# Adjacency loads of a two-layer GNN kernel: partition quadrants 2 and 3 issued by ScalarE instead of SyncE

## What is computed

```python
def reference(x, adj, L0_gnn_w, L1_gnn_W, L1_gnn_b):
    # layer 0
    A = adj + eye(N)
    d = rsqrt(sum(A, axis=1))
    h = elu(((A * d[:, None] * d[None, :]) @ x) @ L0_gnn_w)
    x = layernorm(x + h)
    # layer 1
    h = relu((adj @ x) @ L1_gnn_W.T + L1_gnn_b)
    return layernorm(x + h)
```

## Time and profile before

| | |
|---|---|
| median of 3 runs | 950.19 us (949.61 to 953.15) |
| the profiled execution, first to last instruction (its span) | 945.9 us |
| time outside the span (median less span) | 4.3 us |
| TensorE busy | 798.6 us, 84% of the span |
| VectorE busy | 736.0 us, 78% |
| ScalarE busy | 530.9 us, 56% |
| GpSimd busy | 101.9 us, 11% |
| granted TensorE clock, mean | 0.951 of full speed |
| moved by DMA | 190.08 MB, mean 201 GB/s |
| SP's queue | 187312 packets, 185.23 MB |

### The profile page before, as it was taken

One profiled execution on the slowest core, in us unless ns is written; L12 is line 12 of the kernel. 1 busy time (PEld: TensorE's weight loads), 2 busy tenths in 40 slices (PEclk: granted clock), 3 DMA queues, 4 the chain that ended last, 5 costly groups with the idle time before them and its releaser, 6 DMA issues. The chain is left out here.

```text
span 945.9 us, 10551 instructions
## 1 busy us (share of the span) xinstructions
PE 798.6 (84%) x3524; PEld 656.8 (69%) x3524; DVE 736.0 (78%) x537; ACT 530.9 (56%) x1192; POOL 101.9 (11%) x108
## 2 busy tenths in 40 slices
PE   0151756569989999999999999999999999999993
PEld 0041635457768888888888888888887778888882
DVE  0454636579979878989898898988987979888861
ACT  2153535367777764475676757667573665455352
POOL 0000000000000000021110211202110231122020
PEclk9995777788999999999999999999999999999997
DMA  9999999999999999998999999999999799998900
GB/s 215 221 219 221 221 220 220 221 225 238 228 230 227 203 206 216 208 219 180 199 209 197 201 207 193 212 191 220 195 211 212 171 211 209 219 219 181 198 23 22
DMA packets 191972, 190.08 MB, mean 201 GB/s; under 512 B 6960, under 2 KB 191920, under 8 KB 191920
## 3 DMA queue, kind: packets, MB, share of 16 engines
q1 hardware_dynamic: 187312, 185.23, 96.2%
q10 hardware_dynamic: 4608, 4.20, 1.5%
HBM read 185.20 MB, written 4.19 MB: 200 GB/s over the span
## 5 line engine op out<-in xcount | busy, mean ns | idle before, releaser
L710 PE MATMUL acc<-a_hi,v_hi 128*128 128x512 f32 x1024 | 411.7, 402 | 35.6 <-DVE a_lo L496 31.4
L343 ACT ACTIVATE a_hi<-turned 128x1024 fp32r<-128x1024 f32 x256 | 265.2, 1058 | 309.5 <-DVE turned L479 151.6
L711 PE MATMUL acc<-a_lo,v_hi 128*128 128x512 f32 x1024 | 406.3, 397 | 0.0
L712 PE MATMUL acc<-a_hi,v_lo 128*128 128x512 f32 x1024 | 406.0, 396 | 0.0
L479 DVE STREAM_TRANSPOSE turned<-raw 128x2048 f32<-128x2048 f32 x128 | 294.1, 2305 | 85.2 <-DMA raw<-in_adj_dram 78.6
L496 DVE TENSOR_TENSOR a_lo<-turned,a_hi 128x1024 fp32r<-128x1024 f32 x256 | 301.4, 1215 | 23.4 <-ACT a_hi L343 15.0
L710 PEld LDWEIGHTS acc<-a_hi,v_hi 128*128 128x128 f32 x1024 | 197.3, 193 | 80.3 <-issue 28.7
L712 PEld LDWEIGHTS acc<-a_hi,v_lo 128*128 128x128 f32 x1024 | 196.9, 192 | 42.3
L711 PEld LDWEIGHTS acc<-a_lo,v_hi 128*128 128x128 f32 x1024 | 197.4, 193 | 40.7
L353 ACT ACTIVATE acc<-raw 128x256 f32<-128x256 f32 x236 | 86.8, 368 | 47.1 <-DMA raw<-in_adj_dram 47.1
L503 DVE TENSOR_REDUCE deg_parts<-raw 128x10 f32<-128x2560 f32 (+4 forms) x32 | 78.1, 2444 | 27.0 <-DMA raw<-in_adj_dram 27.0
(11 more groups left out here) (43 smaller groups left out, 347.3 us busy)
## 6 DMA issues: line engine op xcount, KB each, us to landing
raw<-in_adj_dram SPq DMA_DIRECT2D x336, 512.0 KB, 10.4
x_row<-in_x_dram SPq DMA_DIRECT2D x64, 128.0 KB, 9.3
out_dram<-normed ACTq DMA_DIRECT2D x32, 128.0 KB, 2.7
w_sb<-in_L_gnn_w_dram SPq DMA_DIRECT2D x1, 256.0 KB, 12.4
normed<-in_L_gnn_W_dram SPq DMA_DIRECT2D x1, 256.0 KB, 10.7
b_sb<-in_L_gnn_b_dram SPq DMA_DIRECT2D x1, 128.0 KB, 10.1
```

The lines of the kernel that those rows point to most:

```text
L343: nc.scalar.activation(a_hi[u % 2][:, part, :], turned[u % 2][:, part, :], ACT.Copy).then_inc(s_hi, 1)
L710: pe.matmul(dst, v_hi[:, k, ch], a_hi[u % 2][:, t, :], start=begin, stop=False)
L711: pe.matmul(dst, v_hi[:, k, ch], a_lo[u % 2][:, t, :], start=False, stop=False)
L712: ins = pe.matmul(dst, v_lo[:, k, ch], a_hi[u % 2][:, t, :], start=False, stop=end)
```

## The change

ScalarE gets the loads of quadrants 2 and 3 of every chunk. SP keeps quadrants 0 and 1, and the weights and `x`. For the chunks whose buffer is free from the start ScalarE issues at once. Otherwise it waits with `raw_free` itself: in stages B and C just ahead of `hi` of the chunk's last unit, in stage A behind its own `deg_part`. The order of quadrants on SP changes from 0, 2, 1, 3 to 0, 1.

```diff
@@ SP
                 if before[n] is not None:
                     raw_free(sp, before[n])
-                load_chunk(sp, n, (0, 2, 1, 3))
+                load_chunk(sp, n, (0, 1))
@@ ACT
+            def load_after(n):
+
+                raw_free(act, n)
+                if n in after:
+                    load_chunk(act, after[n], (2, 3))
+
+            for n in range(len(chunks)):
+                if before[n] is None:
+                    load_chunk(act, n, (2, 3))
             for n, (name, row, panel, mine) in enumerate(chunks):
                 last = n // PANELS - 1
                 for u in mine:
+                    if name != "A" and u == mine[-1]:
+                        load_after(n)
                     hi(u)
...
                 if name == "A":
                     raw_loaded(act, n)
                     deg_part(n)
+                    load_after(n)
```

## The result

The changed kernel takes 901.79 us in the median of 4 runs (896.89 to 905.3), the kernel before 951.67 on the same chip (949.61 to 953.61, 4 runs). The ratio is 0.948, with a 95% interval of 0.945 to 0.952: 5.2% faster, 49.9 us between the medians. The profiled execution of the changed kernel is the longest of its four, 905.3 us with a span of 903.3. Between the two spans lie 42.6 us, and it is these that the traces can explain.

A forecast was written before the change was run, and what follows sets the result against it. Transfers were taken to bound roughly the first 219 us, PE nearly all after. Stage A -57, issues +2 and stage C -2 gave -57: about 889 us of span, 893 with 4.3 outside it, 895 with 2 for PE's clock; range 870 to 928.

The forecast's parts named there:

- What bounds the kernel: Whole kernel: transfers bound roughly the first 219 us, at about 220 GB/s, and PE nearly everything after.
- Why 220 GB/s: Adjacency loads: the 32 partitions each fills hold the rate at 220 GB/s, not packet size or HBM; 128-partition loads reach 343.
- Stage A by rows: Stage A: at 343 GB/s while both queues have work, its eight rows take 285 us against 342, -57 us.
- the term for the time in which a queue has no work: Stage A, rows 1 to 3: 4 us added to each row's 26, as x loads on SP hold back its half.
- The issues on ACT: ACT's 168 adjacency loads: 0.49 us each, 82 us in all, mostly covered; estimate +2 us.
- The cover: Stages B and C: ACT's halves already wait 1.4 us each for PE, more than a pair of issues at 0.98.
- The added waits: ACT's waits before loading: nothing in B and C; in A nothing, at most 2 us x 8, with `keep_xt` up to 2.8 us later.
- Stage C: Stage C: chunks with one unit starve PE; faster landing gives back about 2 us.
- PE's clock: Early rows, clock 0.71 to 0.79: 2 us allowed because it may not rise as bursts close up.
- the queues serialise: Rival for both load queues: packets cost as much as at 220 GB/s, rows stay 40 us, 950 us; chance 0.09.
- Partial overlap: Rival for the load queues: they fall out of step, mean about 260 GB/s, -27, 923 us; chance 0.10.
- ACT's queue blocked: Rival for ACT's issues: a pair costs 4.4 us before `hi`, +97, 1047 us; decides above 2.5 us a pair; chance 0.06.

The follow-up runs named there:

- same-half run: Changed kernel with SP loading quadrants 0 then 2 and ACT 1 then 3, so both queues meet in one half; 941.52 us, ratio 0.989 to the kernel before.

## Why the prediction was right, and where it was off

**What bounds the kernel: right.** Rows 0 to 4 were bound by transfers, the rest by PE. The change in B and C alone does nothing (952.98 us), the change in A alone everything (904.21). The windows of the earlier trace rows were not all cut at the degree sums, though the prediction says so; rows 1 to 4 took 39.5, 36.3, 45.1 and 44.2 us, not 40 to 43 each. Their sum is the same.

**Why 220 GB/s: right, and shown.** That the partitions written hold the rate, not packets, engines or memory, rested on one stretch of 1.5 us in the earlier trace rows. In the changed kernel both queues together reach the same number for longer, here a stretch of 5 us:

```profile
10.00:15.00 5.00, 0.00 (x0) 0.00 (x0) 0.00 (x0) 3.78 (x13) 0.00 (x0) 1.00 1.10 347
```

The same-half run makes it sharper: what holds the rate is the half, since two quadrants of one half at once get 208 GB/s.

**Stage A by rows: right in kind, too large in size.** The forecast was -57 us, the spans show -42.6, of which 41.9 in stage A. The full rate was right. What was mis-sized is the term for the time in which a queue has no work: nothing but 0.6 in row 0, where 6.5 were lost (44.9 against 38.4), 4 us in row 3, where about 10 were (35.8 against 26), and nothing in row 4, which took 38.2 against a forecast of 33. Row 4 had been taken as bound by PE, with 29.7 us and 3 more. Cut at its degree sums, it had 32.5 us of PE in the kernel before; in the changed one PE works 28.9 us of it and is idle for 9. Rows 1 and 2 came within 0.7 us, in part by luck: the wait for the projection, to which the 4 us were put down, is worth 4.8 us in row 1, but only 1.0 in row 2, which had taken 36.3 us and not 40.5. Of the misses, the run with the x loads later takes away 5.1 us in row 4, and only 1.9 in row 3. Row 3 then still takes 33.9 us with PE busy 25.5 of 34, at 283 GB/s. The changed kernel's trace shows what row 3 waits for. First ACT's copy of the transposed x (`keep_xt`), then two windows (columns as above):

```profile
114.67 1.02 ACT L372 ACTIVATE x_row<-proj 128x1024 f32<-128x1024 f32 x1 [10.19 <-PE proj L660]
...
115.00:117.00 2.00, 1.25 (x6) 1.12 (x7) 2.00 (x2) 2.00 (x8) 0.00 (x0) 1.00 0.54 149
117.00:119.00 2.00, 2.00 (x11) 1.77 (x10) 1.62 (x1) 1.48 (x8) 0.00 (x0) 1.00 0.03 12
```

ACT stands 10.19 us in `keep_xt`, behind the products that PE does before the transposition. Only then does it sum the next chunk, whose buffer neither queue may fill before that, and both run dry: ACT asks again at 118.59 us, SP, behind the projection and x, at 121.34. The run with the x loads later has the same wait, 8.64 us, and 77 GB/s from 111 to 113 us. From 121 to 133 us the changed kernel moves 214 to 243 GB/s, with mostly one queue at work. By these rates the dry stretch (115 to 121 us) costs about 4 us and the single queue another 4 (estimates), together most of row 3's 10. No run takes this wait away. Row 6 came 2.3 us shorter than forecast.

**The issues on ACT: right.** 366 and 474 ns were measured against 490, and PE's work in B and C took as long as before: 359.7 of 360 us busy in the first window, with 1.9 us of waits for `a_lo` where it was 1.8. The cover was another than named: ACT's waits for PE stayed (121.7 us against 118.8), its waits for the turned unit shrank (41.9 against 77.7). DVE waits 15.5 us for `a_hi` in place of 12.4, off PE's path. That SP's long issues in stage A were a full queue is borne out, as SP's own median there fell from 2189 to 484 ns once its queue carried half.

**The added waits: not nothing.** `keep_xt` was to come up to 2.8 us later at no cost; in row 3 it holds ACT for 10.19 us, and with it the loads, as above. The wait for DVE's `deg_part` was written off because DVE is ahead of ACT. At the start it is not, since it stands behind the weights, and ACT loses 13.46 us. The run with the weights first took this wait away and gained nothing, with SP's half of the first chunk behind the weights; what it costs by itself is open.

**Stage C: not seen.** PE is busy 223.3 of 227 us where it was 222.5: 0.8 us against the 2 forecast, within what the runs can't tell.

**PE's clock.** 2 us were allowed for a clock that might not rise. The granted clock rose a little, from 0.951 to 0.966 in the mean of the two traces.

**The rivals.** That the queues serialise is refuted: 0.948. The Trainium skill's page "DMA: Bandwidth & Descriptors", section "Issuing engines are not separate DMA queues", says that issuing from several engines saves only the time of issuing, and its rules for kernel authors say that transfers to disjoint partition halves serialise. The runs disagree where each load fills only 32 partitions and the two queues write different halves (347 GB/s against 220); where both write the same half, the second queue indeed brings nothing (208 GB/s). Partial overlap, as a mechanism, was part of the truth (the run with opposite halves in turn, at 920.88 us, comes near its 923): the mean rates of rows 1 to 4 are 262 to 294 GB/s rather than 343, and most of the 15 us between the 285 and the 299.7 is there and in row 0. ACT's queue blocked at the start, where two of its first six issues took 4.16 and 2.88 us. From 40 us on an issue took 1.43 us at most and 0.37 to 0.47 us in the median, so a pair took under 1 us, where 2.5 would have decided.

**The sum.** 895 forecast, 901.8 measured, inside 870 to 928. (The lower end was written as 871; 950.19 less 78 is 872.) The profiled execution stands 2.0 us above its span, and not 4.3 as taken from the median of before. That gap set the median of several executions beside the span of one, so scatter was in it: single executions of the changed kernel range from 896.89 to 905.3 us.

## What to carry to other kernels

Read what a rate depends on before adding queues: one stretch in which another shape of load ran at 343 GB/s beside 219 said both that there was room and where. If loads fill only some partitions, give each queue its own half for good, because queues drift apart: alternating halves gained 31 us, fixed ones 50. And once a load is split over two queues, whatever waits in one of them holds half of every load behind it; moving one wait by one chunk was worth another 11 us. The same holds for whatever the issuing engine itself waits for: ACT's 10 us for a transposition left both queues empty.

## What the runs showed of the hardware beyond what was expected

While the queues have work, the busy share of the DMA engines says nothing of room here: it reads 1.12 at 208 GB/s, 1.11 at 302 and 1.10 at 347.

The rate of both queues together came to 344 to 350 GB/s in many stretches of 5 us and not above, close to the 343 of the 128-partition loads.

Two queues with loads on different halves do not always run together. ACT issued two loads at 127.28 us, and from 127.5 to 130 us only SP's queue moved data (q10, ACT's, has no line):

```profile
127.28 0.90 ACTq L237 DMA_DIRECT2D raw<-in_adj_dram  x2
...
q1 hardware_dynamic: 542, 0.54, 112.1%
```

Until 131 us the rate is about 220 GB/s. The cause is open.
